# Expert results kept by token place instead of by batch, and the image stage's tokens taken one step earlier

## The reference, cut to what matters

```python
h = tok_ref(x, ...)                      # 64 images of 3x96x96: 36 patches each, 5 projections -> 128, layernorm
h = jnp.concatenate([h, txt], axis=1)    # + 77 text tokens: (64, 113, 128)
h = h + attn_ref(_layernorm(h), ...)     # 8 heads of 64, probabilities in bf16
h = h + ffn_ref(_layernorm(h), ...)      # shared expert + 3 of 16 routed experts per token
# in ffn_ref: sigmoid(x @ gate_w.T) + expert_bias -> top 3; each expert: swiglu(x @ gate_up.T) @ down.T
# routed_out = sum over the 3 chosen of gating * expert_out
```

## Time and profile before

| what | us |
|---|---|
| median of 3 runs (lowest, highest) | 796.66 (795.38, 796.78) |
| the profiled execution | 800.95 |
| its span, first to last instruction | 799.1 |

### The profile page before, as it was taken

The page is one execution under the profiler, slowest core; times in us unless marked ns, Lnnn a source line. Parts: engine busy times, 40 slices in busy tenths (PEclk is TensorE's granted clock), DMA queues, the critical chain, the costliest instruction groups (busy, mean ns, idle before and its releaser), DMA issues. The chain is left out here.

```text
span 799.1 us, 20169 instructions
## 1 busy us (share of the span) xinstructions
PE 632.9 (79%) x6122; PEld 535.0 (67%) x6122; DVE 574.5 (72%) x2094; ACT 433.2 (54%) x1044; POOL 547.8 (69%) x696
## 2 busy tenths in 40 slices
PE   6767899999999999999999869773999888772000
PEld 4545788888888888888887657553887677561000
DVE  0697889999999999999999737352666555552244
ACT  2546778888888888888888523221333333220000
POOL 4364122787888878787777877776777777777464
PEclk9978999999999999999999859976999999996555
DMA  9910000001111011111111345555767566780797
GB/s 321 243 56 19 1 2 2 31 31 38 34 34 37 31 34 34 34 33 37 34 34 35 86 125 148 152 152 146 208 205 208 168 192 192 233 271 22 208 326 208
DMA packets 66444, 88.02 MB, mean 110 GB/s; under 512 B 11612, under 2 KB 58848, under 8 KB 66186
## 3 DMA queue, kind: packets, MB, share of 16 engines
q1 hardware_dynamic: 30420, 34.76, 15.8%
q10 hardware_dynamic: 23824, 28.68, 12.3%
q0 software_dynamic: 12096, 23.30, 8.7%
HBM read 57.32 MB, written 30.87 MB: 110 GB/s over the span
## 5 line engine op out<-in xcount | busy, mean ns | idle before, releaser
L611 POOL DMA_INDIRECT dispatched<-pay,sloti x192 | 204.2, 1064 | 58.3 <-issue 49.6
L630 POOL DMA_INDIRECT expert_rows<-yb,dst_i x186 | 182.0, 979 | 60.7 <-issue 51.4
L1055 ACT ACTIVATE xe<-bank 128x256 f32<-128x256 f32 x93 | 35.7, 384 | 151.9 <-PE bank L883 141.5
L688 PE MATMUL bank<-xt,wqkv 128*128 128x452 f32 x384 | 101.4, 395 | 6.3 <-issue 5.1
L1453 DVE TENSOR_TENSOR hide<-bank,sge 128x256 f32<-128x256 f32 x93 | 39.3, 422 | 72.5 <-ACT sge L1060 41.0
L688 PEld LDWEIGHTS bank<-xt,wqkv 128*128 128x128 f32 x384 | 68.8, 196 | 13.0 <-issue 7.1
L837 PE MATMUL bank<-kt,qt 64*113 64x113 f32 x1024 | 68.1, 273 | 4.7 <-DVE h L1345 4.7
L894 PE MATMUL bank<-xe,kt 128*128 128x256 f32 (+1 forms) x296 | 66.9, 355 | 5.0 <-issue 4.6
L784 PEld LDWEIGHTS bank<-wo_r,ot 128*113 128x113 f32 x512 | 62.4, 184 | 7.2 <-ACT ot L982 3.4
L1027 ACT ACTIVATE s<-bank 113x452 bf16<-113x452 f32 x128 | 63.0, 549 | 6.3 <-PE bank L837 6.3
L837 PEld LDWEIGHTS bank<-kt,qt 64*113 64x113 f32 x1024 | 56.7, 177 | 12.3 <-issue 6.2
(11 more groups left out here) (210 smaller groups left out, 1760.1 us busy)
## 6 DMA issues: line engine op xcount, KB each, us to landing
kt<-in_w_ffn ACTq DMA_DIRECT2D x74, 192.0 KB
xs_all<-dispatched SPq DMA_DIRECT2D x77, 140.0 KB
x2t<-expert_rows SPq DMA_DIRECT2D x16, 672.0 KB
vr<-in_w_ffn ACTq DMA_DIRECT2D x35, 192.0 KB
out_h<-h ACTq DMA_DIRECT2D x16, 224.0 KB
x2t<-in_x ACTq DMA_DIRECT2D x4, 864.0 KB, 9.4
x2t<-in_x SPq DMA_DIRECT2D x4, 864.0 KB, 10.4
dispatched<-pay,sloti POOLq DMA_INDIRECT x192
```

The source lines that it names most:

```text
L611: pool.indirect_dma_start(out=xs_dram[:, :], out_offset=bass.IndirectOffsetOnAxis(ap=sloti[:, q % (PAYS // GRP), b, c:c + 1], axis=0), in_ ...
L630: pool.indirect_dma_start(out=y_dram[:, :], out_offset=bass.IndirectOffsetOnAxis(ap=dst_i[:, slot, j:j + 1], axis=0), in_=yb[t % RW][:, j, ...
L688: m = nc.tensor.matmul(dst, wqkv[:, a, at:at + 128], xg[:, b, :], start=(j == 0), stop=(j == 2))
```

## The change

Two edits. First, the row in `expert_rows` becomes `(t * 64 + b) * 3 + k`: rows of one token place lie together over all batches. The table `dest0`, the offset added for each group and the view through which the results are read follow. The number and the sizes of the scatters stay. The DMA that reads a group now finds 4 x 3 rows of one token place next to each other. The rows of neighbouring token places of one batch, 1,536 bytes apart before, are 64 x 1,536 = 98,304 bytes apart.

```diff
-            yv = y_dram.rearrange("(b t k) d -> t b k d", t=T, k=TOPK)
+            yv = y_dram.rearrange("(t b k) d -> t b k d", t=T, k=TOPK)
...
-            nc.gpsimd.iota(dest_i[:, :, :], pattern=[[T * TOPK, GRP], [1, TOPK]], base=0, channel_multiplier=TOPK).then_inc(S["iota_set"], 1)
+            nc.gpsimd.iota(dest_i[:, :, :], pattern=[[TOPK, GRP], [1, TOPK]], base=0, channel_multiplier=B * TOPK).then_inc(S["iota_set"], 1)
...
-                nc.gpsimd.tensor_scalar(pay[0:T, at, DESTS], dest0[0:T, :, :], float(q * GRP * T * TOPK - NY), None,
+                nc.gpsimd.tensor_scalar(pay[0:T, at, DESTS], dest0[0:T, :, :], float(q * GRP * TOPK - NY), None,
```

```diff
             for o in range(NOCT):
                 shifted(o)
+                tokens(o)
                 if o + 2 < NOCT:
                     features(o + 2)
-                tokens(o)
...
             for o in range(NOCT):
                 shifts(o)
-                if o >= 1:
-                    biased(o - 1)
+                biased(o)
                 if o >= 2:
                     scaled(o - 2)
-            biased(NOCT - 1)
```

## The result

The changed kernel is slower: 801.41 us (median of 22 runs, 798.28 to 805.15) against 797.64 us (22 runs, 794.50 to 804.03) for the kernel before beside it. The ratio is 1.0041 with a 95% interval of 1.0021 to 1.0060. The forecast was 792.3 with a range of 786.5 to 799.0; its sign was wrong. The profiled execution took 802.74 us, its span 800.2. The ratios use runs in the fast state alone.

The account below looks back on a forecast made before the run. The prediction took DMA packet time to bound the combining stage. Reads -4.0, scatters 0 and image stage -0.4 gave -4.4 us: 796.5 us for the profiled execution, 792.3 for the median, range 786.5 to 799.0.

Parts of the forecast that it names:

- The bound: Combining stage: limited by the DMA engines' time for packets, 2.72 us per group at a share of 1.10.
- Reads, -4.0 us: Combining stage: 6,144-byte packets at 238 ns replace four of 77, token 112 on one engine; a group takes 2.51 us.
- 308 and more: Combining stage: ns per large read packet that would show the forecast wrong; about 240 would show it right.
- The turns: Combining stage: engines take turns by packet, reads run ahead and last additions hide behind queued outputs; up to 3 us gained.
- the first rival: Combining stage: all large reads at 238 ns, -8.2 us in all, 788.5 us, or 785.5 with turns by packet; chance 0.21.
- Slower: the pitch: Combining stage: streams 98,304 bytes apart meet on the same part of memory, packets take 361 ns, 801.0 us; chance 0.12.
- The packets were not the price: Combining stage: 6,144 bytes still take 308 ns, leaving only the image-stage gain, 796.3 us; chance 0.15.
- the rule on spreading: Combining stage: by the skill page, token 112's single-row DMA would spread over 16 engines, giving the low end.
- Scatters, 0: Expert tiles: scatters to places 98,304 bytes apart cost nothing more; bounds 0 and 3 us at the last scatter.
- Edit 2, -0.4 us: Image stage: reordered TensorE and ScalarE work brings GpSimd's addition to 28.4 from 28.79; bounds -1.0 and +1.5 us.
- the step from the addition to the landing: Image stage: octet 0's rows land in `h` behind GpSimd's addition and start VectorE's rounds, so 0.4 us earlier carries through.
- The added wait for the bias: Image stage: TensorE waits 0.6 us more per octet, covered by idling for image data; uncovered it would cost 4.8 us.

Follow-up runs that it names:

- e5: Kernel before, but ScalarE issues no output until the last group is combined, so reads of 1,536 bytes run alone; ratio 1.0163.
- e1: Changed kernel with the layout lines taken back, leaving only the new image-stage order; 797.68 us, ratio 1.0013 to the kernel before.
- e2: Kernel before with only the new layout of `expert_rows`, image stage in its old order; 804.71 us, ratio 1.0079.
- e14: The new layout alone against the kernel before, on a slower chip; 907.17 us, ratio 1.0078.
- e3: Changed kernel with gaps in the ring buffers, cutting each read packet into four of 1,536 bytes; 797.69 us, ratio 0.9993 to the kernel before.
- e15: Changed kernel with outputs written in packets of 2,048 bytes, 7 per engine and group; 799.73 us, ratio 1.0015 to the kernel before.
- e16: Kernel before with outputs in packets of 2,048 bytes, so 28 read packets against 7 output packets; 804.73 us, ratio 1.0069.
- e11: Changed kernel with read packets of 3,072 bytes and the image stage in its old order; 799.00 us, ratio 0.9991 to the kernel before.
- e13: The changed kernel once more, against the kernel before on a slower chip; 907.92 us, ratio 1.0063.
- e4: Changed kernel, but SP issues a group's read only when the output of five groups earlier has landed; 808.62 us, ratio 1.0136 to the kernel before.
- e9: Changed kernel with SP issuing outputs too, so large reads and outputs share one queue; 803.57 us, ratio 1.0053 to the kernel before.
- e10: Kernel before with SP issuing outputs too, so reads of 1,536 bytes and outputs share one queue; 804.21 us, ratio 1.0053.

## Why the prediction was wrong

**The bound.** It took the DMA engines' share of 1.10 for engines full of their own work, so that a cheaper packet would show. We infer that the share counts the time for which packets are under way, waiting included. Reads alone fill it too, at 109.1%, and move 250 GB/s (e5), against 363 with outputs between (e1). A share over 100% is not only an overlap of two queues, as was said ahead of the prediction: one queue alone shows 104.6% and 109.1%. The row that said so was on the table: 90 ns per read with no output beside it, 77 with the earlier trace rows. The prediction noted it as an argument for a rival and still priced the packet by itself. (Its counts also took the 4-byte packets that end a DMA for data: 4,977 packets with 7.33 MB hold about 4,770 of 1,536 bytes.)

**Reads, -4.0 us: the step that failed.** It priced 6,144 bytes at 238 ns, from image loads in which nothing flows the other way. Here the reads of the changed kernel took 0.874 x 480 us for 7.44 MB, 346 ns per 6,144 bytes by the same reckoning of share, against 322 ns for four small ones (0.799 x 480 us for 7.33 MB). "308 and more" was the prediction's own sign of being wrong. A group took 2.91 us instead of 2.51. The other half of this step was right: it supposed that one engine carries the row of token 112 whole, and the packet counts show that. With its own formula and 346 ns, that engine would need (8 x 346 + 29 x 29.7) / 1.10 = 3.30 us per group to keep up with the outputs; 2.91 was measured, and there the outputs fell behind. Measured, both edits together are +0.41%, 3.3 us of 797.64, and the layout alone +0.79% and +0.78% (e2, e14). Why the large packet is no cheaper here stays open.

**The turns.** The prediction named this mechanism, in the first rival: by turns of a packet, seven reads against 28 outputs, reads run ahead. It gave it the wrong sign, a gain of up to 3 us by hiding the last additions behind queued outputs. Reads did get ahead, but a group took longer, not shorter, and behind the last combination the outputs run alone at 207 GB/s. The Trainium skill (DMA: Bandwidth & Descriptors, section Queues, rings and completion order) says that each DMA engine goes round the queues that have work, a whole packet at a time. The runs fit that without showing it: equal counts lose 0.15% or nothing that can be told (e3, e15), 7 against 28 and 28 against 7 lose 0.4 to 0.8% (changed, e2, e16), but 14 against 28 loses nothing (e11), and the single row explains part of this as well.

**The rivals.** "Slower: the pitch" had nearly the right time, 801.0, by the wrong cause, and that is luck: e3 keeps the pitch and loses nothing. The Trainium skill (DMA: Bandwidth & Descriptors, section Latency and other measured facts) lists losses for row pitches of 2 MiB and more and next to none at 512 KiB; it does not list this pitch, and e3's 0.9993 is in line with it. "The packets were not the price" was right on the reads' rate and missed the outputs. By the rule on spreading that the prediction took from the Trainium skill (DMA: Bandwidth & Descriptors, section Why a DMA increments its semaphore by 16 and not by 1) the single row would have been spread over 16 engines. Measured, it stayed on one (17 ends per group, not 32).

**Scatters, 0: right.** 14.1% of the engines' time from 560 to 640 us against 14.0%, and VectorE's wait for buffers 33.4 us against 33.1.

**Edit 2, -0.4 us: the number came out by luck.** In the timeline of the changed kernel (columns as in the earlier trace rows) the rows of octet 0 are ready earlier, and the stage ends 0.33 us earlier, at 55.41 instead of 55.74:

```profile
26.80 1.26 POOL L539 TENSOR_TENSOR xs_all<-xs_all,tgb 72x512 f32<-72x512 f32 x1 [0.99 <-ACT xs_all L955]
...
36.47 1.64 DVE L1095 BATCH_NORM_STATS2 st<-h 113x6 f32<-113x128 f32 x8 [7.18 <-DMA h<-xs_all]
...
55.41 0.35 DVE L1312 TENSOR_SCALAR xn<-h,mean,rs 113x128 f32<-113x128 f32 x1
```

GpSimd's addition came 2.0 us earlier than in the earlier trace rows. The profiles of all the kernels show what of this is the edit. With the old order (seven profiles) that addition starts at 27.9 to 28.8 us, with the new one (eleven) at 26.8 to 28.0: about 1 us earlier, more than the 0.4 forecast. But what starts VectorE's rounds, the landing of octet 0's rows, came at 36.7 to 38.7 with the old order and at 36.5 to 41.3 with the new, and the first attention step at 55.4 to 57.3 and at 55.4 to 59.6. So the step that failed is the one from the addition to the landing: the landing did not follow, and why was not looked into. The added wait for the bias shows as 0.59 us before each L669 and is covered, as computed. No timed run can tell so little (e1; e13 beside e14).

## What to carry to other kernels

Before making one stream's DMA packets larger, look at what shares the engines with it from another queue. In these runs packet counts of 28 and 28, 14 and 28, and 7 and 7 went with no loss that could be told, and 7 against 28 in either direction with 0.4 to 0.8%. That the turns of the queues are the cause is not shown. Look also at how many engines carry what: the leftover row that became one large packet went to one engine here, and a group is complete only when that engine is done. The packet counts of a queue show it. A DMA share of 100% doesn't say that the engines' own work is the limit; compare the rate of one direction alone with that of both. An issue of a DMA that suddenly lasts microseconds is a sign that its queue has fallen behind.

## What the runs showed that was not expected

Reads from DRAM into 112 partitions (and the single row) alone reach 250 GB/s (1,536-byte packets) to 279 (6,144), 512-byte outputs alone 195 to 207, and small ones of both together 324 to 363: much of the second direction comes free. Holding back one side for the other (e4, 266 GB/s, 1.4% slower) or putting both in one queue (e9, e10, 0.53% slower) is worse than two queues of like packets. And a change of how a DMA is cut also changed how many engines its smallest part used, which none of the expectations had taken up.
